# A routing merge with the picks as the fixed operand, in four column groups, and exponentials kept in PSUM

## What is computed

```python
logits = jnp.einsum('bsd,ed->bse', x, gate_w) + gate_b
probs = jax.nn.softmax(logits, axis=-2)          # over the tokens
vals_t, idx_t = jax.lax.top_k(probs.transpose(0, 2, 1), K)
...
merged = jnp.einsum('bked,bke->bed', tok, vals)
```

## Time and profile before

| | us |
|---|---|
| median of 3 runs | 1333.97 |
| lowest and highest run | 1333.05, 1335.24 |
| profiled execution, its own time | 1337.08 |
| span in the profile (first to last instruction) | 1335.4 |
| PE busy | 1290.5 (97%) |
| DVE busy | 1045.1 (78%) |
| ACT busy | 951.0 (71%) |
| POOL busy | 317.8 (24%) |
| routing, up to PE's first `turn_q` | 83.4 |

### The profile page before, as it was taken

One profiled execution on the slowest core, in us unless ns is written; L12 is line 12 of the kernel. 1 busy time (PEld: TensorE's weight loads), 2 busy tenths in 40 slices (PEclk: granted clock), 3 DMA queues, 4 the chain that ended last, 5 costly groups with the idle time before them and its releaser, 6 DMA issues. The chain is left out here.

```text
span 1335.4 us, 32264 instructions
## 1 busy us (share of the span) xinstructions
PE 1290.5 (97%) x11493; PEld 1079.6 (81%) x11493; DVE 1045.1 (78%) x3340; ACT 951.0 (71%) x2384; POOL 317.8 (24%) x694
## 2 busy tenths in 40 slices
PE   5989999999999999999999999999999789999999
PEld 3678888787978888797888878888887578888888
DVE  6768986898698778868986888788688857767673
ACT  5759885889598778959895987689598724444333
POOL 4524231332222313222322233132223200000000
PEclk9789999999999999999999999999999999999999
DMA  5543232332323322322322233233222322112100
GB/s 211 181 155 109 74 114 80 95 133 75 104 75 114 99 78 100 105 89 89 120 95 91 87 104 110 68 110 105 89 88 86 102 75 65 56 56 56 56 17 32
DMA packets 90831, 125.18 MB, mean 94 GB/s; under 512 B 8760, under 2 KB 77104, under 8 KB 90672
## 3 DMA queue, kind: packets, MB, share of 16 engines
q1 hardware_dynamic: 90352, 123.11, 28.7%
q10 hardware_dynamic: 320, 0.00, 0.0%
HBM read 103.69 MB, written 19.40 MB: 92 GB/s over the span
## 5 line engine op out<-in xcount | busy, mean ns | idle before, releaser
L1213 ACT ACTIVATE prob<-prob,low 128x512 f32<-128x512 f32 (+3 forms) x512 | 281.0, 552 | 104.1 <-DVE low L1374 104.0
L1374 DVE CUSTOM_DVE_ANT_0 prob<-at,mask 128x512 f32<-128x512 f32 (+3 forms) x512 | 219.7, 485 | 8.9 <-PE at L960 8.9
L947 PE MATMUL at<-w_hi,c_lo 128*128 128x386 f32 x512 | 188.0, 367 | 1.3 <-DVE area_raw L1319 1.3
L947 PE MATMUL at<-w_lo,c_hi 128*128 128x386 f32 x512 | 174.2, 340 | 0.0
L947 PE MATMUL at<-w_hi,c_hi 128*128 128x386 f32 x512 | 174.0, 340 | 0.0
L1387 DVE TENSOR_SCALAR prob<-prob,rec 128x512 f32<-128x512 f32 (+3 forms) x512 | 169.9, 395 | 4.5
L999 PE MATMUL at<-ident,prob 128*128 128x128 f32 x1280 | 164.4, 275 | 3.3 <-DVE low L1374 1.9
L1027 PE MATMUL at<-probT,v 128*32 128x512 f32 (+3 forms) x2048 | 151.1, 435 | 4.6 <-DVE probT L1397 2.6
L999 PEld LDWEIGHTS at<-ident,prob 128*128 128x128 f32 x1280 | 142.3, 140 | 10.7 <-issue 1.6
L1524 POOL TENSOR_TENSOR area_sq<-area_sq 128x512 f32<-128x512 f32 x64 | 82.2, 1285 | 242.2 <-ACT area_sq L1177 242.2
L1027 PEld LDWEIGHTS at<-probT,v 128*32 128x32 f32 x2048 | 63.2, 109 | 92.3 <-issue 82.2
(11 more groups left out here) (265 smaller groups left out, 3238.0 us busy)
## 6 DMA issues: line engine op xcount, KB each, us to landing
area_w<-in_L_ffn_w SPq DMA_DIRECT2D x65, 1024.0 KB, 5.6
bias<-in_L_ffn_w SPq DMA_DIRECT2D x160, 32.0 KB, 4.5
x_in<-in_L_attn_x SPq DMA_DIRECT2D x8, 512.0 KB, 5.6
xr<-in_L_attn_x SPq DMA_DIRECT2D x8, 512.0 KB, 4.6
eo_d<-hidT SPq DMA_DIRECT2D x32, 128.0 KB, 1.8
x_d<-xr SPq DMA_DIRECT2D x8, 512.0 KB, 2.8
area_raw<-x_d SPq DMA_DIRECT2D x8, 512.0 KB, 3.9
out<-area_raw SPq DMA_DIRECT2D x7, 512.0 KB, 3.1
```

The source lines that it names most:

```text
L947: m = eng.matmul(bQ[n % 2][:, 0:W], a[:, (j // HP) % 2, k, n * P:(n + 1) * P], w[:, k, j % HP, :], start=start, stop=(k == KC - 1 and a is ...
L1213: eng.activation(sl, sl, ACT.Exp, scale=-1.0, bias=low[:, i:i + 1], accum_out=den[:, i:i + 1]).then_inc(exp_done.sem, 1)
L1374: eng.tensor_tensor_reduce(out=prob[s % 2][h][:, off[c]:off[c + 1]], in0=bC[i][:, at:at + (c + 1) * P], in1=mask[:, (NT - 1 - c) * P:T], s ...
```

## The change

The merge swaps its operands. For each of the four groups of tokens, the picks (128 tokens x 32 experts) are the weights and the 256 channels of the normed tokens move past them. The four results are not accumulated: each goes to its own 32 partitions, and so its own 32 columns of the array. Group `n`'s partial sum stands in partitions `32n` to `32n+31`, experts on the partitions. `copy_part` on DVE copies the 128 x 256 values into SBUF (`part`), and `add_parts` on PE multiplies `part` (as weights, 128 x 128 for each half of the channels) with `stack`, a 128 x 32 matrix of four unit matrices one under the other, which adds the four groups and turns the result in one. `copy_merged` on ACT is as before but waits for `add_parts`. `stack` is made once, by a reduction over the identity on DVE. The exponentials move from an SBUF tile to partitions 32 to 63 of the logits' bank. The expert's picks, logits and everything behind `merged` are the same.

```diff
+        ("part", [P, C], F32),
+        ("stack", [P, E], F32),
-        ("expd", [E, T], F32),
...
+    expd = bL[E:2 * E, :]
...
+            for n in range(NT):
+                m = eng.matmul(bank_of(b)[n * E:(n + 1) * E, KC * E:KC * E + C], pickT_of(b)[:, n, :], xn[b % SLOTS][:, n, :],
+                               start=True, stop=True)
+            m.then_inc(pe_merged.sem, 1)
+
+        def add_parts(b):
+            eng.wait_ge(merged_done.sem, merged_done.at(b, 1))
             for k in range(KC):
-                for n in range(NT):
-                    m = eng.matmul(bank_of(b)[:, k * E:(k + 1) * E], xn[b % SLOTS][:, n, k * P:(k + 1) * P], pickT_of(b)[:, n, :],
-                                   start=(n == 0), stop=(n == NT - 1))
+                m = eng.matmul(bank_of(b)[:, k * E:(k + 1) * E], part[:, k * P:(k + 1) * P], stack[:, :], start=True, stop=True)
             m.then_inc(pe_merged.sem, 1)
...
             if b == 5:
                 gate_keys()
+            if 0 < b < B - 1:
+                add_parts(b - 1)
             if b + 1 < B:
                 gate(b + 1)
...
         merge(B - 2)
+        add_parts(B - 2)
         merge(B - 1)
+        add_parts(B - 1)
...
-            eng.activation(expd[:, :], logits[:, b % 2, :], ACT.Exp, bias=nmax[:, 0:1],
+            eng.activation(expd, logits[:, b % 2, :], ACT.Exp, bias=nmax[:, 0:1],
...
+        def copy_part(b):
+            eng.wait_ge(pe_merged.sem, pe_merged.at(b, 1))
+            eng.tensor_copy(part[:, :], bank_of(b)[:, KC * E:KC * E + C]).then_inc(merged_done.sem, 1)
...
+        eng.tensor_reduce(stack[:, :], ident.rearrange("p (j e) -> p e j", e=E), AX.X, ALU.add).then_inc(gate_copied.sem, 1)
         moments(0)
...
             choose(b)
             if b + 1 < B:
                 split_low(b + 1)
+            if 0 < b < B - 1:
+                copy_part(b - 1)
             if b == 5:
                 copy_keys()
             weigh(b)
...
+        copy_part(B - 2)
+        copy_part(B - 1)
```

More of the change, by code:

```diff
@@ L229, in route_tokens @@
     x, xn = [tiles[f"x_in{u}"] for u in range(SLOTS)], [tiles[f"xn_{u}"] for u in range(SLOTS)]
-    logits, top8, left, nmax, expd, den, rden, pick, pickT = (tiles[k] for k in (
-        "logits", "top8", "left", "nmax", "expd", "den", "rden", "pick", "pickT"))
+    logits, top8, left, nmax, den, rden, pick, pickT = (tiles[k] for k in (
+        "logits", "top8", "left", "nmax", "den", "rden", "pick", "pickT"))
     raw_w, u_in, u_blk, u_sq, u_half, tmp, ss, slope, om, e0, l0, gk, qk_w, qaug32 = (tiles[k] for k in (
@@ L238, in route_tokens @@
     bT, bL, bP, bM = (bank[2:4], bank[4:6]), bank[6], bank[7][:, 0:P], bank[7][:, P:]
+    expd = bL[E:2 * E, :]
+    part, stack = tiles["part"], tiles["stack"]
     ev = lambda name, per, unit=1: Signal(ctx, nc, "r_" + name, per, unit)
-    gate_load, gate_t, gate_copied = ev("gate_load", 2, 16), ev("gate_t", 1), ev("gate_copied", 2)
+    gate_load, gate_t, gate_copied = ev("gate_load", 2, 16), ev("gate_t", 1), ev("gate_copied", 3)
     load = [ev(f"load{u}", 1, 16) for u in range(SLOTS)]
@@ L249, in route_tokens @@
     kept_done, pick_done, merged_done, pickT_done = (
-        ev("kept_done", 1), ev("pick_done", 1), ev("merged_done", 1), ev("pickT_done", 1))
-    pe_xT, pe_gate, pe_pickT, pe_merged = ev("pe_xT", KC), ev("pe_gate", 1), ev("pe_pickT", 1), ev("pe_merged", 1)
+        ev("kept_done", 1), ev("pick_done", 1), ev("merged_done", 2), ev("pickT_done", 1))
+    pe_xT, pe_gate, pe_pickT, pe_merged = ev("pe_xT", KC), ev("pe_gate", 1), ev("pe_pickT", 1), ev("pe_merged", 2)
     logits_done, exp_done, w_hi_done, w_lo_done = ev("logits_done", 1), ev("exp_done", 1), ev("w_hi_done", 1), ev("w_lo_done", 1)
@@ L426, in norm @@
             eng.wait_ge(shift_done.sem, shift_done.at(b))
-            eng.wait_ge(pe_merged.sem, pe_merged.at(b - SLOTS))
+            eng.wait_ge(pe_merged.sem, pe_merged.at(b - SLOTS, 1))
             for n in range(NT):
@@ L455, in copy_pick @@
             if b < B - 1:
-                eng.wait_ge(pe_merged.sem, pe_merged.at(b - 1))
+                eng.wait_ge(pe_merged.sem, pe_merged.at(b - 1, 1))
             else:
@@ L591, in weigh @@
             eng.wait_ge(left_done.sem, left_done.at(b))
-            eng.scalar_tensor_tensor(left[:, :], left[:, :], LOWEST / 2, expd[:, :],
+            eng.scalar_tensor_tensor(left[:, :], left[:, :], LOWEST / 2, expd,
                                      ALU.is_le, ALU.mult).then_inc(kept_done.sem, 1)
@@ L654, in vector @@
         eng.tensor_copy(gT_hi[:, :, :], grid).then_inc(gate_copied.sem, 1)
-        eng.wait_ge(gate_copied.sem, gate_copied.at(0, 1))
+        eng.wait_ge(gate_copied.sem, gate_copied.at(0, 2))
         eng.tensor_tensor(gT_lo[:, :, :], grid, gT_hi[:, :, :].bitcast(F32), ALU.subtract).then_inc(gate_copied.sem, 1)
```

## The result

| | before | changed |
|---|---|---|
| median of the runs | 1333.61 us (1333.05 to 1335.24, 4 runs) | 1343.09 us (1342.46 to 1344.54, 4 runs) |
| profiled execution, own time | 1337.08 | 1343.66 |
| its span | 1335.4 | 1341.6 |
| mean granted clock of TensorE in it | 0.988 | 0.986 |
| `turn_q` starts, end of routing | 83.44 | 88.21 |

The changed kernel is slower: ratio 1.0061, 95% interval 1.0043 to 1.0079. A later set of runs gave 1343.02 against 1335.18 us, 1.0066 (1.0051 to 1.0081). The forecast was 1339.2 us with a range of 1334.0 to 1343.3: the sign is right, the value lies 0.2 us inside the upper edge.

A forecast was written before the change was run, and what follows sets the result against it. Routing was taken as bound by ACT's copies at 2.4 GHz and PE at 1.2 GHz, in turn. Terms summed to +5.2 us: 1342.3 against the profiled execution, 1339.2 against the median of 1333.97; range 1334.0 to 1343.3.

The forecast's parts named there:

- round 1: Routing round 1: late `add_parts` at the lower clock delays ACT by 2.8 us, partly absorbed by an earlier wait; +2.1 us.
- round 2: Routing round 2, all at the lower clock: `norm` follows 4.9 us after the round's start instead of 5.5; -0.6 us.
- rounds 3 and 4: Routing rounds 3 and 4: `copy_merged` waits for the late copy and `add_parts`, delaying `norm` on ACT; +1.2 us each.
- round 5: Routing round 5: `gate(6)` comes early, so waits of 0.91 and 0.33 us go; -1.2 us.
- round 6, to `merge(6)`: Routing round 6: `gate(7)` waits about 1 us for copy and `add_parts`, earlier logits return over half; +0.4 us.
- the end, `merge(6)` to `turn_q`: End of routing: DVE's `ssq` and the norm's chain wait for both last copies; +1.65 us.
- behind it: After `turn_q`: a longer stretch at 1.2 GHz following PE's idle time of about 2.7 us; +0.4 us.
- The mechanism: Rounds 1 to 6: `copy_merged` on ACT waits some 2 us for `add_parts`, since `copy_part` stands behind `split_low` on DVE.
- The new products: Merge's first half on PE: four column groups run side by side, 0.43 us at full clock, 0.85 at the lower.
- The falling clock: Rival, chance 0.22: PE stays at 1.2 GHz through rounds 3 to 6, 3.6 us more, 1342.8 us.
- The rising clock: Rival, chance 0.22: rounds 1, 2 and round 6's projections run at 2.4 GHz; +2.3 us, 1336.3 us.
- The faster case: Rival, chance 0.10: `copy_part` slips in early, ACT's 4.8 us of merge waits go for 0.5 at the end; 1329.7 us.

The follow-up runs named there:

- part_first: Changed kernel with `copy_part(b-1)` ahead of `split_low(b+1)` on DVE; 1337.25 us, ratio 0.9999 to the kernel before.
- keep_busy: Changed kernel plus four unused identity products on PE in rounds 1 to 5, just ahead of `add_parts`; 1343.10 us, ratio 1.0053 to the kernel before.
- before_busy: Kernel before plus four unused identity products on PE in rounds 1 to 5, ahead of the next gate; 1334.00 us, ratio 0.9993.
- all_three: Changed kernel with `copy_part` ahead of `split_low`, `copy_merged` behind `norm`, and sequences 6 and 7 merged the old way; 1334.23 us, ratio 0.9986 to the kernel before.
- before_late: Kernel before, old merge, with `copy_merged(b-1)` moved behind `norm(b+2)` on ACT; 1335.30 us, ratio 0.9998.
- exp_only: Kernel before with only the exponentials moved to the logits' bank in PSUM, old merge kept; 1333.75 us, ratio 0.9983.
- best_again: Second set of runs of all_three, on the same chip as the changed kernel; 1333.90 us, ratio 0.9991 to the kernel before.

## Why the prediction was right in sign, and 3.9 us short

Measured between the two recorded profiles, the sum holds up to `turn_q`, though not in every term: round 1 was put too high by about as much as the start of round 1 and round 6 together were put too low.

| term | predicted | measured |
|---|---|---|
| start of round 1 | 0 | +0.85 (23.90 to 24.75) |
| round 1 | +2.1 | +0.33 (9.08 to 9.41) |
| round 2 | -0.6 | -0.84 (9.26 to 8.42) |
| rounds 3 and 4 | +1.2 each | +1.32, +1.36 |
| round 5 | -1.2 | -1.41 (9.04 to 7.63) |
| round 6, to `merge(6)` | +0.4 | +1.47 (14.11 to 15.58) |
| the end, `merge(6)` to `turn_q` | +1.65 | +1.69 (4.50 to 6.19) |
| to `turn_q` together | +4.75 | +4.77 |
| behind it | +0.4 | +1.8 |
| own time of the profiled execution | +5.2 | +6.6 |

- **The mechanism** was right: `copy_merged` waits 2.2 us a round for `copy_part` and `add_parts`, DVE's order is the reason, and an exchange of two steps there gives 5.9 us back (part_first).
- **The end** was right: `ssq` came 2.79 us after `merge(6)` began and not 1.09, so 1.70 later against 1.6 in the text.
- **The new products** run side by side, as `gate_keys` did. The next product on PE started 0.57 us after the first (42.73 to 43.30), and DVE's copy 0.70 after it at the end. I took 0.43. The page "TensorE: Matmul & The Clock Gate" of the Trainium skill, section "Measured speedup vs the span model", gives 2.38 times for three column tiles; the estimate from it was 0.54. What was 0.57 includes the change to `turn_wk`'s weights, so the rows don't decide between them; only the two last merges stand on the path, where it comes to some 0.1 us each.
- **Round 1** was too dear by 1.8 us: I let PE stay at the lower clock there, and the window shows 1.00. 0.85 of it came in ahead of the round, where the starts scatter between 23.4 and 25.0 in all the profiles. That the sum to `turn_q` came out within 0.02 us is luck in these terms.
- **Round 6** was too cheap by 1.1 us. `add_parts` and the copy made `gate(7)` 0.5 us later (3.94 against 3.47 after the round's start); then the six products of the gate took 2.54 us and not 1.53, at 0.43 us each, for the clock was down after PE's 2.29 us of waiting. In the earlier trace rows the same thing was to be seen in round 1.
- **Behind `turn_q`** the measured +1.8 is 1.4 us in the span and 0.4 outside it. The forecast's reason, a longer stretch at 1.2 GHz, shows: the first 5 us behind `turn_q` had a granted clock of 0.56 against 0.68. But this part of the span differs by 2.5 us among the fourteen profiles, so the 1.4 proves nothing.
- **The step that failed** is the last one of the sum: "against the median of 1333.97 it gives 1339.2". The terms of rounds 2 and 5, -0.6 and -1.2, exist only against a profile in which the old merge runs at the lower clock there. That profile's execution was 3.1 us above the median, and I carried its sum over to the median unchanged. The high clock makes the kernel before faster (1333.2 us at 0.994 to 0.995). The changed kernel took 1341.9 to 1344.7 us in all its ten executions, at 0.985 to 0.989; what it does at 0.994 is known only from the one execution of keep_busy, 1341.3. Round by round against before_busy, whose rounds run at the full clock, rounds 1 to 5 cost 1.28, 1.54, 1.30, 1.18 and 0.84, the start 0.73 and the rest 2.84: 9.7 us at `turn_q` (88.21 - 78.50). The median of the change is +9.5 us for that reason; against the kernel before at a clock of 0.986 to 0.988 it is +4.9. The 3.1 us were written down in front of me, and the two windows at 0.50 and 0.63 pointed at them (the first of them begins in round 1; cut where ACT's rounds begin, rounds 2 and 5 have 0.50 and 0.62). For the median the gains in rounds 2 and 5 should have been taken off and the +1.2 of the rounds at full clock put there in their place: 5.2 + 1.8 + 2.4 = 9.4 us, an estimate from the prediction's own terms.
- **The range** held the result, by luck: its upper end was the falling clock's 1342.8 with 0.5 added, and that case did not come about.
- **The falling clock**, a rival with 0.22, gave 1342.8 and would pass for right by its number. It is not the main cause: rounds of 8.11 and 8.12 us at 1.00 and 0.77 say so, and the execution of keep_busy at 0.994. In round 6 it added 1.0 us, and in round 2 perhaps 0.3 (8.42 us at 0.59 against 8.11 in round 3). **The rising clock** (1336.3) came in round 1 alone (1.00); round 2 had 0.59, and the first of the projections in round 6 ran at the lower clock as before. **The faster case** asked that `part` be ready before the exponentials are done. In the changed kernel it isn't (the exponentials were done at 44.34 in round 3, `part` at 45.72). all_three comes near to it, and the result is level with the kernel before, not ahead of it by what the rival promised; before_late shows that the waits it wanted to save were worth nothing that the runs can tell.

## What to carry to other kernels

Cut a long step of one engine into pieces with a copy between them only where the copy has a place in the other engine's order as early as its input is ready: here the product was finished 1.9 us before DVE reached the copy, and the time lost was the place in the queue, not the 0.4 us of the instruction. And before a sum is carried from one profile to a median, compare the granted clock of the stretch with that of the other executions: a gain that exists only in windows of low clock has to be taken off when the runs have a high one.

## What was unexpected of the hardware

The spread of the kernel before, 1331.9 to 1341.5 us, goes with whether TensorE falls to 1.2 GHz in some rounds of the first 80 us; the rest of the program takes 1251.9 to 1254.4 us behind `turn_q` in all fourteen profiles. None of the executions above 1338 us was profiled, so that their long time lies in routing too is not shown. Four products a round whose result nobody reads, 1.06 us of PE in a round, keep the clock up in the old kernel. The Trainium skill, page "TensorE: Matmul & The Clock Gate", section "What's actually happening", says of the ramp to the full clock that it costs under 1% of a typical span and that one should not fit to a count of slow products. The runs agree in size, with 0.7% between their ends, though the low stretches here come in the middle of routing; for a change that was worth 0.4 to 0.7%, that is the size of the effect itself.

DVE's product of the thresholded logits with the exponentials reads two inputs. With both in SBUF it took 0.66 us alone, but longer wherever it ran beside GpSimd's split of the weights. In before_busy, GpSimd from 34.54 for 2.20 us, and DVE:

```profile
34.54 2.20 POOL L532 TENSOR_TENSOR w_lo<-raw_w,w_hi 128x1024 fp32r<-128x1024 f32 x1
```

```profile
35.67 1.61 DVE L602 SCALAR_TENSOR_TENSOR left<-left,expd 32x512 f32<-32x512 f32 x1
```

In exp_only, with the exponentials in PSUM, beside the same work:

```profile
33.72 2.19 POOL L522 TENSOR_TENSOR w_lo<-raw_w,w_hi 128x1024 fp32r<-128x1024 f32 x1
```

```profile
35.09 0.68 DVE L592 SCALAR_TENSOR_TENSOR left<-left,at 32x512 f32<-32x512 f32 x1
```

The first took 1.34 to 1.83 us in five of its eight executions in before_busy, each beside such a split. It ended 0.54 us after GpSimd did (37.28 and 36.74), so it seems to have waited for it and then run. The small instruction in best_again's round 6, 128x16 with two inputs in SBUF, shows it more plainly: 2.08 us in place of 0.17, ended 0.04 us after GpSimd's. The second took 0.68 each time in every kernel that has the exponentials in PSUM. The Trainium skill's page "SBUF — State Buffer", section "Terms", describes a pair of ports that VectorE and GpSimd lock in turn, the loser blocked; the trace agrees, and shows that one input in PSUM was enough to escape it here. DVE was not the bound of these rounds, so it brought no time that the runs can tell. Nor is it what makes best_again's rounds shorter: exp_only has the exponentials in PSUM too, and its rounds 2 and 3, at 1.00, took 6.76 us each, as rounds 3 and 4 of the recorded profile did with them in SBUF (6.79 and 6.76).
